# Third layer rebuilt: sixteen 32x32 conditioning products, fp32 expert products on two row halves, first group's routing between the second layer's last products

## What is computed

```python
def cond(x, embedding, ...):            # third and fourth layer
    att = softmax(mlp(embedding))       # 64 x 8
    agg_w = einsum('bk,koi->boi', att, weight)   # 32 x 32 for each batch
    return einsum('boi,bih->boh', agg_w, x) + (att @ bias_k)[:, :, None]

def ffn_2(c):                           # third layer
    logits = c @ router_weight.T + router_bias   # 64 experts
    scores = softmax(logits); keep the 8 largest as w_dense, their sum as w_sum
    return c * w_sum + w_dense @ expert_bias     # 64 x 512

def ffn_3(c):                           # fourth layer, 8 experts
    routing = softmax(c @ gate_w.T)
    return (c * (routing @ in_scale)) @ sign(weight).T * (routing @ out_scale) + bias
```

## Time and profile before

| | us |
|---|---|
| median of 3 runs | 559.41 (558.78 to 559.51) |
| the profiled execution, its time | 561.05 |
| its span in the profile | 559.2 |
| base(3), the last of the second layer, starts | 423.96 |
| the third layer's stretch, up to router3(0) | to 494.3 |

### The profile page before, as it was taken

The page is one execution under the profiler, slowest core; times in us unless marked ns, Lnnn a source line. Parts: engine busy times, 40 slices in busy tenths (PEclk is TensorE's granted clock), DMA queues, the critical chain, the costliest instruction groups (busy, mean ns, idle before and its releaser), DMA issues.

```text
span 559.2 us, 7216 instructions
## 1 busy us (share of the span) xinstructions
PE 545.5 (98%) x2697; PEld 420.2 (75%) x2697; DVE 254.6 (46%) x530; ACT 129.9 (23%) x227; POOL 192.7 (34%) x176
## 2 busy tenths in 40 slices
PE   7999999999999999999999999999999999989997
PEld 5788888888888888888888876353535699966784
DVE  3443233622123522226322427172543378897775
ACT  4322222322223222223222221000020022234332
POOL 2499992400001300001104700210002044489986
PEclk9999999999999999999999999999999999999999
DMA  9298430195000310000304006999921333120413
GB/s 308 95 420 306 132 99 0 55 153 111 0 0 0 100 69 0 0 0 1 94 16 119 1 0 87 159 126 223 157 87 20 91 98 94 19 33 7 148 56 118
DMA packets 84357, 50.34 MB, mean 90 GB/s; under 512 B 69616, under 2 KB 74736, under 8 KB 83568
## 3 DMA queue, kind: packets, MB, share of 16 engines
q1 hardware_dynamic: 82240, 38.97, 32.0%
q0 software_dynamic: 2016, 11.01, 5.5%
q10 hardware_dynamic: 80, 0.08, 0.0%
HBM read 31.93 MB, written 8.62 MB: 73 GB/s over the span
## 4 chain that ended last, share of the span: by engine, by line
PE 89%; DVE 5%; DMA 2%; issue 2%; ACT 1%; SPq 0%; DVEq 0%
PE ps L550 88%; DMA xs<-in_x 2%; DVE c_lo L973 1%; DVE cT L973 1%; ACT c_hi L859 1%; DVE rest L1155 0%; DVE t L973 0%; DVE c_lo_odd L973 0%; PE ps L734 0%; DVE xs L973 0%; PE ps L790 0%; PE ps L740 0%; DVE wcat L973 0%; PE ps L696 0%; DVE m L1151 0%
## 5 line engine op out<-in xcount | busy, mean ns | idle before, releaser
L550 PE MATMUL ps<-c_lo,wl 128*128 128x512 f32 x448 | 173.0, 390 | 0.2
L550 PE MATMUL ps<-c_hi,wl 128*128 128x512 f32 x448 | 172.9, 390 | 0.1
L973 DVE TENSOR_TENSOR hff<-silu,ps 128x512 f32<-128x512 f32 x56 | 38.5, 688 | 161.9 <-PE ps L550 161.9
L550 PEld LDWEIGHTS ps<-c_lo,wl 128*128 128x128 f32 x448 | 84.1, 188 | 18.5 <-POOL c_lo L425 0.6
L550 PEld LDWEIGHTS ps<-c_hi,wl 128*128 128x128 f32 x448 | 84.0, 188 | 18.0 <-ACT c_hi L859 0.7
L550 PE MATMUL ps<-wl,h_hi 128*128 128x512 f32 x224 | 87.7, 391 | 0.0
L550 PE MATMUL ps<-wl,h_lo 128*128 128x512 f32 x224 | 87.2, 389 | 0.0
L425 POOL TENSOR_TENSOR c_lo<-cT,c_hi 128x512 fp32r<-128x512 f32 x8 | 10.6, 1327 | 158.7 <-ACT c_hi L859 158.6
L973 DVE TENSOR_TENSOR h_lo<-hff,h_hi 128x512 fp32r<-128x512 f32 x56 | 47.4, 847 | 39.1 <-ACT h_hi L859 39.1
L859 ACT ACTIVATE h_hi<-hff 128x512 fp32r<-128x512 f32 x56 | 35.4, 632 | 112.5 <-DVE hff L973 112.5
L893 ACT ACTIVATE silu<-ps 128x512 f32<-128x512 f32 x56 | 33.5, 598 | 116.2 <-PE ps L550 116.2
(11 more groups left out here) (163 smaller groups left out, 632.7 us busy)
## 6 DMA issues: line engine op xcount, KB each, us to landing
wl<-in_wl POOLq DMA_DIRECT2D x14, 768.0 KB, 10.0
stg<-y_dram SPq DMA_DIRECT2D x64, 128.0 KB, 5.1
xs<-in_x SPq DMA_DIRECT2D x4, 1024.0 KB, 8.2
x_all<-in_x SPq DMA_DIRECT2D x1, 4096.0 KB, 14.9
y_dram<-prod SPq DMA_DIRECT2D x16, 256.0 KB, 2.2
xs<-x_all SPq DMA_DIRECT2D x4, 1024.0 KB, 4.9
bias_bc<-bias_dram SPq DMA_DIRECT2D x15, 256.0 KB, 5.2
out_x<-x_all SPq DMA_DIRECT2D x15, 256.0 KB, 2.0
```

The source lines that it names most:

```text
L550: return pe.matmul(o, l, r, start=start, stop=stop)
L973: return dve.tensor_tensor(o, a, b, op)
```

## The change

- **Conditioning.** `mix_rows` uses each batch's 32 x 32 matrix as weights and 32 partitions of a staged x as moving data of 512 columns: 16 products a group, one for each of the 16 places of the array. The result has rows on partitions. The staged x (`xT`) needs another order of rows (slot in the group on the partition quarter), so SP writes x to DRAM (`spill`) and reads it in four DMAs (`fetch`); the attention masks are built by five GpSimd operations at the kernel's start, and the bias becomes a column (`biasN`) that ScalarE adds (`rows_out`, into `cS`).
- **Turning.** `turn_c` makes the turned c for the router, VectorE copies it (`store_c`) into `cT`; the transposes back are gone.
- **Router.** Eight products of 64 x 256 on two column tiles; ScalarE adds the router's bias, `turn_logits2` turns logits.
- **Experts.** `wcat` is one fp32 value for each weight; two transposes; four fp32 products on 64 rows each, into banks 5, 6, 7 and g.
- **Scaled c.** ScalarE scales `cS` in place, and a GpSimd DMA that accumulates adds it to `x_all` after `final2`. GpSimd's additions are gone.
- **Order.** `last1` puts group 0's conditioning, turning, router and logits between the pieces of `base(3)`, and group 1's conditioning after `lora_b`. The third layer is unrolled. Groups 1 and 2 have one product of ones by `bias3` into bank 7 that nobody reads. The fourth layer's first two conditionings wait for the accumulating DMAs.

In the diff a "..." behind a removed line stands for more removed lines of the same function, which is printed above.

```diff
+        def order2(g):
+            return tuple((max(g - 1, 0) + n) % GT for n in range(GT))
+        def base2(g):
+            return GT if g == 0 else 0
+        def experts_bank(g, j):
+            return bank((5, 6, 7, g)[j])
+        def cT2(g):
+            return cS[G - 1] if g == 0 else cT
...
-            def stage(g):
...
+            def spill(g):
+                sp.wait_ge(s_x_new[1], GT * (g + 1))
+                dst = x_dram[g * TOK:(g + 1) * TOK].rearrange("(j p) n -> p j n", p=P)
+                sp.dma_start(dst, x_all[:, g * GT:(g + 1) * GT, :]).then_inc(s_x_dram[g], 16)
+            def fetch(g):
+                sp.wait_ge(s_x_dram[g], 16)
+                if g == 0:
+                    sp.wait_ge(s_cond_mm[1], G * Q)
+                if g == 2:
+                    sp.wait_ge(s_cond_mm[0], G * S)
+                for j in range(GT):
+                    src = x_dram[(g * GT + j) * P:(g * GT + j + 1) * P].rearrange("(b i) n -> i b n", b=TB)
+                    sp.dma_start(xT(g)[j * ROWS:(j + 1) * ROWS], src).then_inc(s_xT[g], 16)
...
-            for g in range(G):
-                stage(g)
-                bias(2, g)
-            for g in range(G):
+            spill(0)
+            spill(1)
+            fetch(0)
+            fetch(1)
+            spill(2)
+            fetch(2)
+            bias(3, 0)
+            spill(3)
+            fetch(3)
+            for g in range(1, G):
...
+            pool.wait_ge(s_pack_b, 16)
+            member = jmask.rearrange("b (g r k) -> b g r k", g=G, k=K)[:, :, :, 0]
+            slot = selrep.rearrange("b (c o) -> b c o", c=TB)[:, :, 0]
+            mask(strip_sum[:, 0:2], member[:, 0:2], member[:, 2:4], ALU.add)
+            two = [strip_sum[:, n].unsqueeze(2).broadcast_to([NB, GT, ROWS]) for n in range(2)]
+            mask(strip2[:], two[0], two[1], ALU.add)
+            rows = member.rearrange("b g r -> b r g")
+            mask(group_sum[:, 0:2], rows[:, 0:2], rows[:, 2:4], ALU.add)
+            mask(group_sum[:, 2], group_sum[:, 0], group_sum[:, 1], ALU.add)
+            mask(place2[:], group_sum[:, 2].unsqueeze(2).broadcast_to([NB, G, TB]),
+                 slot.unsqueeze(1).broadcast_to([NB, G, TB]), ALU.mult)
...
             def add_scaled(g):
-                pool.wait_ge(s_staged[2], (g + 1) * 16)
...
+                pool.wait_ge(s_x_new[2], GT * (g + 1))
+                pool.wait_ge(s_cS_scaled, GT * (g + 1))
+                pool.dma_start(x_all[:, g * GT:(g + 1) * GT, :], cS[g][:], accum_op=ALU.add).then_inc(s_cS_added[g], 16)
+            for g in range(G):
+                add_scaled(g)
...
+            def mix_rows(g, places):
+                for n in places:
+                    j = order2(g)[n]
+                    at = slice(j * ROWS, (j + 1) * ROWS)
+                    if g == 1:
+                        pe.wait_ge(s_x_new[1], GT * (G - 1) + j + 1)
+                    if g >= 2 and n == GT - 1:
+                        pe.wait_ge(s_x_new[2], GT * (g - 1))
+                    for b in range(TB):
+                        ins = mm(bank(base2(g) + j)[b * ROWS:(b + 1) * ROWS], agg[at, 1, g * GT + b], xT(g)[at, b])
+                    ins.then_inc(s_cond_mm[2], 1)
+            def turn_c(g, places=range(GT)):
+                for n in places:
+                    j = order2(g)[n]
+                    pe.wait_ge(s_cS, GT * g + n + 1)
+                    for s in range(S):
+                        ins = pe.transpose(bank(base2(g) + j)[:, cols(s)], cS[g][:, j, cols(s)], ident)
+                    ins.then_inc(s_c_turned, 1)
 
             def router2(g):
-                pe.wait_ge(s_cT[2], S * (g + 1))
-                for j in range(GT):
-                    for s in range(S):
-                        ins = mm(bank(4)[:, j * P:j * P + NPAD], cT[:, s, cols(j)], wr2[:, s], s == 0, s == S - 1)
+                pe.wait_ge(s_cT[2], GT * (g + 1))
+                for s in range(S):
+                    c = cT2(g)[:, s].rearrange("p (a h n) -> p h a n", a=2, h=2)
+                    for h in range(2):
+                        ins = mm(bank(4)[h * E2:(h + 1) * E2, 0:2 * P], wr2[:, s, 0:E2], c[:, h], s == 0, s == S - 1)
                 ins.then_inc(s_router2, 1)
+            def turn_logits2(g):
+                pe.wait_ge(s_lgT2, g + 1)
+                for a in range(2):
+                    ins = pe.transpose(bank(4)[:, (2 + a) * P:(3 + a) * P], lgT2[:, cols(a)], ident)
+                ins.then_inc(s_logits2, 1)
 
             def turn_weights(g):
                 pe.wait_ge(s_wcat, g + 1)
-                for j in range(GT):
-                    ins = pe.transpose(bank(4)[:, cols(j)], wcat[:, j], ident)
+                for a in range(2):
+                    ins = pe.transpose(bank(4)[:, cols(a)], wcat[:, 2 * a:2 * a + 2].rearrange("p j e -> p (j e)"), ident)
                 ins.then_inc(s_wcat_turned, 1)
 
-            def layer2(g, more):
...
+            def experts2(g, a):
                 pe.wait_ge(s_wT2, g + 1)
-                for j in range(GT):
...
+                for h in range(2):
+                    e = slice(h * E2, (h + 1) * E2)
+                    mm(experts_bank(g, 2 * a + h), wT2[e, cols(a)], eb2[e]).then_inc(s_product[2], 1)
+            def last1(g):
+                base(g, (0, 1))
+                pe.wait_ge(s_hm, g + 1)
+                turn_hm(g, 3)
+                pe.wait_ge(s_xT[0], 16 * GT)
+                pe.wait_ge(s_pool_step, MIXED2)
+                mix_rows(0, range(GT))
+                base(g, (2,))
+                turn_c(0)
+                pe.wait_ge(s_hmT, g + 1)
+                base(g, (3,), (0, 1))
+                pe.wait_ge(s_weights23, LOADS23)
+                router2(0)
+                base(g, (3,), (2,))
+                turn_logits2(0)
+                base(g, (3,), (3,))
+                lora_b(g)
+                turn_weights(0)
+                pe.wait_ge(s_xT[1], 16 * GT)
+                mix_rows(1, (0, 1))
+                experts2(0, 0)
+                mix_rows(1, (2, 3))
+                turn_c(1)
+            def layer2(g):
+                if g:
+                    turn_c(g + 1, (0, 1))
+                    pe.wait_ge(s_x_new[2], GT * g)
+                    mm(bank(7), ones[:], bias3[:])
+                    turn_c(g + 1, (2, 3))
+                    turn_weights(g)
+                    experts2(g, 0)
+                pe.wait_ge(s_cT[2], GT * (g + 1) + 1)
+                experts2(g, 1)
+                router2(g + 1)
+                if g + 2 < G:
+                    pe.wait_ge(s_xT[g + 2], 16 * GT)
+                    mix_rows(g + 2, (0, 1, 2))
+                turn_logits2(g + 1)
+                if g + 2 < G:
+                    mix_rows(g + 2, (3,))
+            def last2(g):
+                pe.wait_ge(s_cS_added[0], 16)
+                pe.wait_ge(s_blk[3], 1)
+                for s in ORDER3:
+                    if s == ORDER3[-1]:
+                        pe.wait_ge(s_x_new[2], GT * g)
+                    cond_chunk(3, 0, s, s)
+                turn_weights(g)
+                experts2(g, 0)
+                pe.wait_ge(s_cT[3], 1)
+                experts2(g, 1)
+                router3(0)
...
+            def rows_out(g, places):
+                for n in places:
+                    j = order2(g)[n]
+                    act.wait_ge(s_cond_mm[2], GT * g + n + 1)
+                    act.activation(cS[g][:, j], bank(base2(g) + j), ACT.Identity,
+                                   bias=biasN[:, g * GT + j:g * GT + j + 1]).then_inc(s_cS, 1)
+            def layer2(g):
+                act.wait_ge(s_router2, g + 1)
+                act.activation(lgT2[:], bank(4)[:, 0:2 * P], ACT.Identity, bias=rbT).then_inc(s_lgT2, 1)
+                if 0 < g < G - 1:
+                    rows_out(g + 1, (0, 1))
                 exp(s_shifted2, s_exp2, g, E2)
+                if 0 < g < G - 1:
+                    rows_out(g + 1, (2, 3))
+                act.wait_ge(s_wcat_turned, g + 1)
+                copy(wT2[:], bank(4)[:, 0:2 * P]).then_inc(s_wT2, 1)
+                if g == 0:
+                    rows_out(1, range(GT))
                 act.wait_ge(s_share, g + 1)
-                scaled(g, 0)
...
+                act.wait_ge(s_c_turned, GT * (g + 1))
+                for j in range(GT):
+                    act.activation(cS[g][:, j], cS[g][:, j], ACT.Copy, scale=stat[:, 3, j:j + 1]).then_inc(s_cS_scaled, 1)
+            act.wait_ge(s_biasN, 1)
+            rows_out(0, range(GT))
+            for g in range(G):
+                layer2(g)
...
-            pe.wait_ge(s_x_new[2], 2 * GT)
+                layer1(g)
+            last1(G - 1)
+            for g in range(G - 1):
+                layer2(g)
+            last2(G - 1)
+            pe.wait_ge(s_cS_added[1], 16)
             pe.wait_ge(s_blk[3], 2)
-            for n, (s, b) in enumerate(FIRST3):
...
+            for s in range(S):
+                if s == S - 1:
+                    pe.wait_ge(s_x_new[2], NT)
```

(73 more changed lines are left out.)

250 lines of the change are left out of this document (119 added, 131 removed).

## The result

The changed kernel takes 554.89 us (median of 4 runs, 554.72 to 555.50) against 559.46 for the kernel before on the same chip (4 runs, 558.78 to 559.71). The ratio is 0.9916, with an interval of 0.9903 to 0.9929: 4.6 us faster, where 9.5 were forecast. The profiled run took 554.72, with a span of 552.6.

The account below looks back on a forecast made before the run. TensorE, 89% of the chain with VectorE close behind, was taken as the bound. Four parts gave 69.1 to 69.2 against 79.5 us, 10.3 less; GpSimd's lateness and start-up left net 9.5, so 549.9 us, range 547.5 to 557.

Parts of the forecast that it names:

- GpSimd takes 0.5 back … now the split is about 0.6 late: Fourth layer: GpSimd issues its last DMA after final2(3), so its c_lo split comes 0.6 late; 0.5 us lost.
- A, base(3) to router2(1): Third layer's opening, from base(3)'s start to router2(1)'s start: 30.9 to 31.1 us.
- B, two periods: Two third-layer group periods, decided by TensorE's own list at 9.6 us each against 12.17: 19.2 us.
- C, router2(3) to router3(0): Last group's router to the fourth layer's first router, with route2 and cond3(0)'s adds: 9.1 us.
- D, to the end of scale_in: From router3's start to the end of the fourth layer's first scale_in: 9.7 us, before 9.2.
- start-up: Kernel's start: five mask operations ahead of the weight DMAs, covered; one more full-width attention product, 0.3 us.
- The signs named: Timeline signs, including router2(0) ending inside base(3) near 441.3 and router3(0) near 483.5.
- The 64-wide sums: VectorE's four scalar_tensor_tensor operations with a sum, leading to wcat: 0.2 us each, bounds 0.15 and 0.4.
- Row tiles in series: Rival: row tiles in mixes and expert halves don't overlap; gain down to about 1 us, 555.5; chance 0.18.
- A transfer late: Rival: group 3's fetch or the second accumulation arrives late; 3 to 6 us back, 554.5; chance 0.10.
- TensorE's pace: Rival: small tiles and waits halve TensorE's pace from router2(1) to router3(0); 21 us lost, 570; chance 0.05.
- No change: Rival: row tiles and both kinds of halves serial, 0.2 a tiling change, giving back 9 us; chance 0.04.

Follow-up runs that it names:

- number 1: Changed kernel, with GpSimd starting bias_3(1) only after VectorE has made both c_lo parts of group 0; 549.01 us, ratio 0.9805.
- number 2: Changed kernel, with GpSimd waiting for the end of its own block_diagonal(3, 2) before split_x(0); 548.82 us, ratio 0.9800.
- number 9: Changed kernel, with GpSimd waiting once for its own first bias_3(0) addition behind the last DMA issue; 549.69 us, ratio 0.9823.
- number 5: Kernel before, with two extra GpSimd additions, results unused, between block_diagonal(3, 2) and split_x(0); 559.16 us in one run.
- number 6: As number 5, plus one small 256 KB DMA issued by GpSimd directly ahead of bias_3(0); 566.72 us in one run.
- number 7: Changed kernel, with the last accumulating DMA issued behind split_x(0) instead of ahead of bias_3(0); 551.62 us, ratio 0.9866.
- number 11: As number 7, with one GpSimd pause behind that DMA and without the unread product of ones by bias3; 547.04 us, ratio 0.9774.
- number 10: As number 9, without the product of ones by bias3 that nobody reads; 548.75 us, ratio 0.9803.
- number 3: Kernel before, with the change's five mask operations put ahead of the first weight DMAs, results unused; 559.21 us, ratio 0.9983.

## Why the prediction was right and wrong

**The failed step** is "GpSimd takes 0.5 back … now the split is about 0.6 late". The sign and its place were right: GpSimd had no idle time ahead of its first split. But the step priced GpSimd's half of the split alone, as lateness. The fourth layer gave back 7.7, not 0.5. It went wrong in two places.
- VectorE's half runs at the same time, reads two SBUF operands, and stands behind a GpSimd that has issued a DMA and not paused since. It cost 8.9 us in place of 1.4. Put a pause in (numbers 1, 2, 9) and 5.2 to 6.1 come back (554.89 against 549.69, 549.01, 548.82; as ratios to before 0.9916 against 0.9800 to 0.9823); add the DMA to number 5 and the stall appears (number 6, one run: 566.72 against 559.16); put a pause behind number 7's DMA and its stall goes (number 11). This is shown. That the DMA of group 3 was moved directly ahead of this chain I had written down, and asked only when it lands.
- The lateness itself costs 1.7 by the medians (numbers 10, 11). In the two executions whose clock stayed at 1.000 it is 0.5 to 0.7, what was forecast; the rest is the lower clock of the others, which the prediction had only as a rival for the third layer.

The Trainium skill, "SBUF — State Buffer", Who interferes with whom, says that a VectorE instruction with two SBUF inputs contends with a GpSimd instruction that reads SBUF. The Trainium skill, "SBUF — State Buffer", Summary: rules for kernel authors, adds that the second to issue is blocked until the first finishes. The rows of before agree: 1.36 and 1.77 where the least is 0.68, so at most one GpSimd instruction's wait. After a GpSimd DMA the wait measured went over seven instructions, so there the rule is too mild, and the measurement decides.

**The parts of the sum**, predicted and measured between the same marks:

| part | predicted | measured |
|---|---|---|
| A, base(3) to router2(1) | 30.9 to 31.1 | 29.7 |
| B, two periods | 19.2 | 19.4 |
| C, router2(3) to router3(0) | 9.1 | 9.1 |
| D, to the end of scale_in | 9.7 | 9.3 |
| in all, against 79.5 | −10.3 | −12.0 |
| fourth layer | +0.5 | +7.7 |
| start-up | +0.3 | −0.8 (number 3, not firm) |

The recorded parts add up to 68.9 to 69.1, not 69.1 to 69.2, which alone is 0.1 to 0.2 more gain than was written down. Part A was too dear by 1.3: I let mix(1) go at the pace of residual(1, 3), bank by bank, 4.6 in all, but with its expert pair it took 3.3 (444.90 to 448.16), since nothing was waited for. With the start-up by number 3 the sum is −12.0 + 7.7 − 0.8 = −5.1, against −4.6 measured; with number 9's rest, −12.0 + 2.3 − 0.8 = −10.5 against −10.15 (559.84 − 549.69). The profiled pair has −6.3 (561.05 to 554.72): in the profiled run of before the first conditioning was over 2.4 later than in that of after (21.12 against 18.77). Number 9 lies at 549.7, the time forecast, but by luck, through terms that nearly cancel: the layer's gain was forecast 1.7 too small, the cost of a late GpSimd 1.8 too small, and the start, if number 3 holds, 1.1 too dear.

**The prices.** Sixteen products on row and column tiles: 1.07 against 0.87 taken (bound 3.5). *experts2* 1.92 against 1.74, *router2* 1.88 against 1.74; each has the change of tiling in it, charged 0.1 apart. The period then came out at 9.72 against 9.6. The 64-wide sums, taken at 0.2, occupy VectorE for 2.7 / 16 = 0.17 each, and ScalarE's `wT2` is waited for 0.47 where 0.7 was charged. The signs named held: router2(0) ends inside base(3), at 439.1; router3(0) at 480.0 came earlier than "near 483.5", 2.3 of it through the earlier start.

**The rivals.** Row tiles in series: refuted by the 1.07; the measured time is near that rival's 555.5, by another cause. The Trainium skill, "TensorE: Matmul & The Clock Gate", Measured speedup vs the span model, gives 10.6 times for a 16-tile pack; the estimate of 1.3 a mix by it lies on the other side of the 1.07. The sixteen products here pack 13 times (13.9 / 1.07), and the measurement decides. A transfer late: no wait of TensorE on a DMA between 421 and 490. The page of after, DMA issues with KB each and median us to landing:

```profile
x_all<-cS POOLq DMA_DIRECT2D x4, 1024.0 KB, 7.1
```

The accumulating DMA lands in 7.1, the estimate was 13. TensorE's pace: 1.00 through the whole third layer, so not as that rival had it; but a lower clock behind waits did come one layer later. No change: the ratio's interval excludes it.

**Left open:** what inside the chip keeps VectorE out after a GpSimd DMA; why the clock falls in some executions of a kernel and not in others, and why number 5, with nearly the same waits as number 9 (0.34 and 0.94), keeps 1.00; and the start-up, where runs of one kernel differ by more than the edit does.

## What to carry to other kernels

When an edit moves a DMA on GpSimd's queue, look at what VectorE reads while GpSimd works on without a pause behind it, not only at when the transfer lands. A single wait of GpSimd on its own semaphore behind the DMA costs nothing that could be measured here and removed an 8.9 us stall. And at a point where TensorE already waits, look at the granted clock of every execution before pricing lateness: in the profile of number 9 two waits of 1.4 together stand beside ten microseconds at 0.82, another execution of the same kernel kept 1.000 and took 547.4, and two with 0.994 took 550.5 and 550.8.

## What the runs showed of the hardware

- Behind a DMA issued by GpSimd, and until GpSimd next pauses, a VectorE instruction with two SBUF operands took 8.92 us (after), 9.66 (number 6), 3.67 (number 7) and 3.10 (number 1) in place of 0.7 to 1.8. It came with a transfer of 1 MB and with one of 256 KB, and didn't end with the landing: number 6's DMA was issued at 493.0 and landed in 3.4, and the stall lasted to 510.5. With a pause nine microseconds ahead of the instruction it took 1.37 (number 11).
- Sixteen fp32 products of 32 x 32 weights on 512 columns take 1.07 us, where one product on the whole array takes 0.87: row tiles overlap like column tiles.
- Under the stall, 7.1 us without work, TensorE's granted clock went from 1.00 to 0.50, and with TensorE at work again from 498.22 on the stretch from 500 to 505 still has 0.88.
